# A fused graph and mixture-of-experts layer: routing two places earlier, and the last batch's expert weights fetched only when the expert changes

## The reference

```
xn = layernorm(x)
x  = x + gnn(xn, src, dst, edge_weight) + mix(xn)        # gather by edge, segment sum, linear attention
h  = layernorm(x)
idx = argmax(softmax(h @ gate_w + gate_b))               # one of 8 experts per node
pos = running count of the node within its expert        # kept if pos < C = ceil(1.25 * 12500 / 8)
y   = relu(h @ w1[idx] + b1[idx]) @ w2[idx] + b2[idx]    # 256 -> 1024 -> 256
out = x + where(kept, prob[idx] * y, 0)
```

## Time and profile before

| what | value |
|---|---|
| runs | 2518.9, 2520.43, 2527.71 us |
| median | 2520.43 us |
| the profiled execution | 2522.2 us, of which 2520.3 us lie between its first and last instruction (the span) |
| busy share of the span | PE 82%, DVE 60%, ACT 41%, POOL 72% |
| granted TensorE clock, mean | 0.919 of full speed |
| moved by DMA | 594.32 MB, mean 236 GB/s |
| weight fetches in it | 82 of 1,028 KB and 82 of 1,024 KB |

### The profile page before, as it was taken

One profiled execution on the slowest core, in us unless ns is written; L12 is line 12 of the kernel. 1 busy time (PEld: TensorE's weight loads), 2 busy tenths in 40 slices (PEclk: granted clock), 3 DMA queues, 4 the chain that ended last, 5 costly groups with the idle time before them and its releaser, 6 DMA issues. The chain is left out here.

```text
span 2520.3 us, 42814 instructions
## 1 busy us (share of the span) xinstructions
PE 2056.2 (82%) x12889; PEld 1586.9 (63%) x12889; DVE 1514.9 (60%) x5328; ACT 1036.6 (41%) x2482; POOL 1810.3 (72%) x1888
## 2 busy tenths in 40 slices
PE   0049999994677777899989999998989899796898
PEld 0015656662455556776767777777777777685787
DVE  6676555554457786787646656666556556555233
ACT  4662333331344454553434433443444444342333
POOL 7777777777777777777777777777777777723654
PEclk9968999997788888999989999999999999897999
DMA  9845666664566667777777776777888888775896
GB/s 338 310 142 169 175 173 175 174 174 131 153 197 193 193 198 259 231 240 231 237 229 248 239 229 221 241 236 237 320 280 306 300 316 285 247 260 221 330 349 248
DMA packets 279341, 594.32 MB, mean 236 GB/s; under 512 B 48437, under 2 KB 177214, under 8 KB 256863
## 3 DMA queue, kind: packets, MB, share of 16 engines
q0 software_dynamic: 93168, 256.28, 33.8%
q1 hardware_dynamic: 155553, 284.06, 32.6%
q10 hardware_dynamic: 30390, 51.21, 5.5%
HBM read 506.22 MB, written 87.99 MB: 236 GB/s over the span
## 5 line engine op out<-in xcount | busy, mean ns | idle before, releaser
L931 POOL DMA_INDIRECT rows_sb<-xn_scratch,src_sb x1517 | 1459.0, 962 | 464.2 <-issue 455.8
L1199 PE MATMUL bank<-acc 128*128 128x128 f32 (+1 forms) x2624 | 442.3, 322 | 15.0 <-issue 10.9
L1220 PE MATMUL bank<-acc 128*128 128x256 f32 x1680 | 413.1, 390 | 0.0
L1199 PEld LDWEIGHTS bank<-acc 128*128 128x128 f32 x2624 | 384.9, 204 | 40.8 <-issue 18.6
L1020 PE MATMUL bank<-rows_sb,s_sb 128*24 128x256 f32 x3082 | 225.7, 413 | 202.0 <-DMA rows_sb<-xn_scratch,src_sb 197.4
L1963 ACT ACTIVATE acc<-bank,acc 128x128 f32<-128x128 f32 (+1 forms) x656 | 212.0, 398 | 375.8 <-PE bank L1199 375.7
L1220 PEld LDWEIGHTS bank<-acc 128*128 128x128 f32 x1680 | 313.9, 194 | 49.7 <-issue 0.9
L1484 DVE TENSOR_TENSOR acc<-acc,bank 128x48 f32 x831 | 170.4, 205 | 273.7 <-PE bank L1030 160.4
L1020 PEld LDWEIGHTS bank<-rows_sb,s_sb 128*24 128x24 f32 x3082 | 84.9, 107 | 274.9 <-issue 232.5
L1884 ACT COPY sums<-bank 120x256 f32<-120x256 f32 x208 | 76.5, 368 | 347.2 <-PE bank L1020 347.2
L1915 ACT ACT_TABLE_LOAD x95 | 121.9, 1283 | 194.8 <-PE bank L1109 193.9
(11 more groups left out here) (263 smaller groups left out, 3649.9 us busy)
## 6 DMA issues: line engine op xcount, KB each, us to landing
acc<-ffn_first_in SPq DMA_DIRECT2D x82, 1028.0 KB
acc<-ffn_w_in SPq DMA_DIRECT2D x82, 1024.0 KB
arena<-xn_scratch SPq DMA_DIRECT2D x194, 128.0 KB, 3.2
h_scratch<-arena ACTq DMA_DIRECT2D x97, 256.0 KB
rows_sb<-xn_scratch,src_sb POOLq DMA_INDIRECT x1517
xnt_scratch<-arena SPq DMA_DIRECT2D x97, 128.0 KB, 2.3
arena<-xnt_scratch SPq DMA_DIRECT2D x97, 128.0 KB
arena<-x_in SPq DMA_DIRECT2D x97, 128.0 KB
```

The lines of the kernel that those rows point to most:

```text
L931: pool.indirect_dma_start(out=chunk_row(c), out_offset=None, in_=xn_d, in_offset=bass.IndirectOffsetOnAxis(ap=src_sb[:, c:c + 1], axis=0)) ...
L1199: m = pe.matmul(bank[:, i * tokens:(i + 1) * tokens], w1_sb[k % 2][:, h, f * P:(f + 1) * P], xt[:, k % 2, h, 0:tokens], start=h == 0, stop ...
L1220: m = pe.matmul(bank[:, i * D:(i + 1) * D], hid[:, f, i * P:(i + 1) * P], w2_sb[k % 2][:, f, :], start=False, stop=f == FC - 1 and i == 0)
```

## The change

It has four parts.

1. **Steps.** A tile's steps stand at distances 0, 1, 2, 2, 3, 3, 4, 5 from its entry in place of 0 to 7, and the logits at 6 in place of 8. The row loads on SP move from 2 to 1, the products (step 3) from 3 to 2. On ACT steps 4 and 5 are now in the early part of a place, ahead of the units' relus.
2. **Ticks.** From place 208 on a place takes one tick, except where a batch's sums are made and the place after, which take two; at the sums the first tick stands ahead of them. `last_c` falls from 217 to 215.
3. **Last batch.** Its 18 columns are dealt out in two halves, the first half to the even units and the second to the odd. Units 64 and 65 get their weights from SP as before. For 66 to 81 POOL issues indirect DMAs that read row `expert * 128 + partition`; where the unit two before, which used the same buffer, has the same expert, 1,024 is added to the row, which puts it out of bounds so that nothing is read. DVE works out these rows after `q_ready` and raises `rows_known`.
4. **Kept columns.** Their scatters start at place 209, four a place, and stand ahead of the units' scatters in a place; there are 78 of them.

```
+        STEP_AT = {0: 0, 1: 1, 2: 2, 3: 2, 4: 3, 5: 3, 6: 4, 7: 5}
+        LAP_AT, LOGIT_AT = 3, 6
...
-        chosen_at = [enters[v[-1]] + C_STEPS - 1 for v in routes]
+        chosen_at = [enters[v[-1]] + LOGIT_AT for v in routes]
...
+        def most_ticks(p):
+            return 2 if p < PAIRS or p in sums_at or p - 1 in sums_at else 1
...
-            if ("unit", n - 1) in here or after == len(here):
+            if e_place[n] in sums_at and e_place[n] >= PAIRS and ("unit", n - 1) not in here:
+                here.insert(0, ("unit", n))
+            elif ("unit", n - 1) in here or after == len(here):
...
-        quiet = [p for p in range(PAIRS + 2, last_c + 4) for _ in range(2 + 2 * (p > last_c))]
+        quiet = [p for p in range(PAIRS + 1, last_c + 4) for _ in range(4)]
...
+            def load_new_first(k):
+                col = k - FINAL[0]
+                pool.wait_ge(rows_known, 1)
+                pool.wait_ge(l1_relu, FC * (k - 1))
+                pool.indirect_dma_start(
+                    out=first_sb[k % 2], out_offset=None, in_=ffn_first.rearrange("a p f -> (a p) f"),
+                    in_offset=bass.IndirectOffsetOnAxis(ap=load_row[:, col:col + 1], axis=0),
+                    bounds_check=NE * P - 1, oob_is_err=False).then_inc(new1_ld[k % 2], 16)
...
+                for k in w1_at[p]:
+                    if k in SKIPS:
+                        load_new_first(k)
+                for k in w2_at[p]:
+                    if k in SKIPS:
+                        load_new_second(k)
                 for k in gather_at[p]:
                     gather_unit(k)
...
+                for col in back_at[p]:
+                    scatter_back(col)
                 for k in scatter_at[p]:
                     scatter_unit(k)
-                for col in back_at[p]:
-                    scatter_back(col)
...
+                if b == LAST:
+                    same, row = empty, idf
+                    link(dve.memset(same, 0.0))
+                    link(dve.tensor_scalar(row, expert, float(P), ids[:, 0:1], ALU.mult, ALU.add))
+                    link(dve.tensor_tensor(same[:, 2:n], row[:, 2:n], row[:, 0:n - 2], ALU.is_equal))
+                    link(dve.scalar_tensor_tensor(row, same, float(NE * P), row, ALU.mult, ALU.add))
+                    dve.tensor_single_scalar(load_row[:, 0:n], row, 1.0, ALU.subtract).then_inc(rows_known, 1)
```

More of the change, by code:

```diff
@@ L294, in build @@
         sel = behind(1, 2 * MOST_SLOTS)
+        load_row = behind(1, MOST_SLOTS).bitcast(I32)
         sprb = behind(0, SLOTS)
@@ L509, in queue_value @@
             return sum(i <= b for i in queued)
+        LAST = len(routes) - 1
+        FINAL = [k for k in range(K) if batch_of[k] == LAST]
+        SKIPS = FINAL[2:]
+        assert len(FINAL) % 2 == 0 and LAST in queued
         def small_steps(p, at_end):
@@ L521, in early_steps @@
         def early_steps(p):
-            found = [("logit", t) for t, e in enumerate(enters) if e + 8 == p]
+            found = [("logit", t) for t, e in enumerate(enters) if e + LOGIT_AT == p]
             for b in range(len(routes)):
@@ L546, in build @@
         last_tick = [first_tick[k] + ticks(k) - 1 for k in range(K)]
+        sums_at = [p + 1 for p in chosen_at]
+        def most_ticks(p):
+            return 2 if p < PAIRS or p in sums_at or p - 1 in sums_at else 1
         e_place, time, p = [], 0.0, FIRST_C
-        wanted_at = [slots_at[b] + (4 if slots_at[b] + 4 < PAIRS else 2) for b in batch_of]
+        wanted_at = [min(slots_at[b] + 4, max(slots_at[b] + 2, PAIRS)) for b in batch_of]
         for k, j in e_ticks:
@@ L561, in build @@
                     break
-                if (j > 1 or k == K or p >= wanted) and time >= cost and e_place.count(p) < 2:
+                if (j > 1 or k == K or p >= wanted) and time >= cost and e_place.count(p) < most_ticks(p):
                     time -= cost
@@ L635, in kept_value, with new_value @@
             return 16 * (k // YS + 1)
+        def new_value(k):
+            return 16 * ((k - SKIPS[0]) // 2 + 1)
         def w2_value(k):
@@ L657, in c_steps @@
         def c_steps(p, order):
-            return [(enters.index(p - s), s) for s in order if p - s in enters]
+            return [(enters.index(p - STEP_AT[s]), s) for s in order if p - STEP_AT[s] in enters]
         def first_of(t):
@@ L830, in sync_program @@
                     elif kind == "early":
-                        for t, s in c_steps(k, (2, 0, 3)):
+                        for t, s in c_steps(k, (1, 0)):
                             if s == 0:
                                 load_turned(t)
-                            elif s == 2:
+                            else:
                                 load_rows(t)
-                            elif t + LAP_TILES < T:
-                                load_acc(t + LAP_TILES)
+                        if k - LAP_AT in enters and enters.index(k - LAP_AT) + LAP_TILES < T:
+                            load_acc(enters.index(k - LAP_AT) + LAP_TILES)
                 for k in w1_at[p]:
-                    load_first(k)
+                    if k not in SKIPS:
+                        load_first(k)
                 for k in w2_at[p]:
-                    load_second(k)
+                    if k not in SKIPS:
+                        load_second(k)
                 for k in keep_at[p]:
@@ L975, in scatter_back, with load_new_second @@
                     bounds_check=tokens - 1, oob_is_err=False).then_inc(back_st[s], 16)
+            def load_new_first(k):
[6 more added lines that the diff above has]
+                    bounds_check=NE * P - 1, oob_is_err=False).then_inc(new1_ld[k % 2], 16)
+            def load_new_second(k):
+                col = k - FINAL[0]
+                pool.wait_ge(l2_mm, l1_done(k - 2))
+                pool.indirect_dma_start(
+                    out=flat2(w2_sb[k % 2]), out_offset=None, in_=ffn_w2.rearrange("a p f -> (a p) f"),
+                    in_offset=bass.IndirectOffsetOnAxis(ap=load_row[:, col:col + 1], axis=0),
+                    bounds_check=NE * P - 1, oob_is_err=False).then_inc(new2_ld[k % 2], 16)
             for p in range(PLACES):
@@ L1631, in queue_units @@
                 link(dve.tensor_single_scalar(queue_base, queue_base, float(u1), ALU.max))
-                if u1 > u0:
+                if b == LAST:
+                    half = (u1 - u0) // 2
+                    link(dve.tensor_scalar(sel[:, 0:u1 - u0:2], iota_p[:, u0 + 1:u0 + 1 + half], queue_at, None,
+                                           ALU.is_equal))
+                    dve.tensor_scalar(sel[:, 1:u1 - u0:2], iota_p[:, u0 + 1 + half:u1 + 1], queue_at, None, ALU.is_equal
+                                      ).then_inc(q_selected, 1)
+                elif u1 > u0:
                     dve.tensor_scalar(sel[:, 0:u1 - u0], iota_p[:, u0 + 1:u1 + 1], queue_at, None, ALU.is_equal
@@ L1976, in side_step @@
                 elif kind == "early":
-                    for t, s in c_steps(k, (7,)):
+                    for t, s in c_steps(k, (7, 4, 5)):
                         c_step(t, s)
@@ L1984, in side_step @@
                 elif kind == "late":
-                    for t, s in c_steps(k, (4, 1)):
+                    for t, s in c_steps(k, (1,)):
                         c_step(t, s)
@@ L1990, in scalar_program @@
             for p in range(PLACES):
-                for t, s in c_steps(p, (6, 5)):
+                for t, s in c_steps(p, (6,)):
                     c_step(t, s)
```

30 lines of the change are left out of this document (19 added, 11 removed).

## The result

| | before | after |
|---|---|---|
| median of 20 runs each | 2520.28 us | 2530.35 us (2523.98 to 2536.36) |
| ratio | | 1.0037, 95% interval 1.0028 to 1.0046 |
| the profiled execution, its span | 2522.2, 2520.3 us | 2531.16, 2529.4 us |
| moved by DMA | 594.32 MB | 571.48 MB |

What follows compares the result with a forecast made beforehand. It took POOL as the bound before place 208 and in the last batch. A and B together gain 14.5 us, C costs 7.5, in sum -7: 2513 us, range 2499 to 2531.

Steps and rivals of the forecast that it cites:

- The bound named for the tail: Last batch: POOL binds, at 1.30 us a DMA and seven a unit, 9.1 us against PE's 7.75.
- A: The way to place 208: last pair starts at 2219, last turning at 2231 in place of 2233.55; gain 2.5 us.
- B: The two last routings, up to the last batch's first gather at 2326.1, before 2340.69; gain with A 14.5 us.
- C: The last batch's units, from first gather to end: POOL binds; costs 7.5 us more than before, though 22.6 MB go.
- One sign: Last batch: PE idle 1 to 2 us in every unit, before L1246 or L1270, until unit 78.
- landing takes 2.8: Before place 208: the last row gather, issued at 2216.3, lands in 2.8 us, so the last pair starts at 2219.
- The 17.3 us from sums to table of batch 17: Routing of batch 17: sums to table takes 17.3 us, before 14.3, as DVE has more in between.
- The landing of w1: Last batch, unit 78: 1 MB lands on a nearly empty DMA in 5.5 us, between bounds of 2.8 and 8.8.
- Rival 1: Last batch: POOL doesn't bind and the tail goes at PE's pace, 2502 us; chance 0.22.
- Rival 2: POOL's weight fetches with 8,224-byte row offsets cost 1 us more each, 25 us in all, 2538 us; chance 0.10.
- Rival 3: Squeezed steps stall PE, 2 us a tile over 98 tiles against a slack of 160.7, 2548 us; chance 0.05.
- Rival 4: Out-of-bounds fetches take as long as full ones, so DMA engines bind again beside POOL, about 2522 us; chance 0.08.

Runs made afterwards that it cites:

- few_fetches: The change with POOL issuing only the ten weight fetches that load something, the 22 skipped ones removed; 1.0002 of the kernel before, 2519.5 us.
- rows_first: The change with the last gather of node rows on POOL ahead of the gathers for units 56 and 58; 1.0013 of the kernel before, 2525.8 us.
- dyn_old_steps: The change with last-batch weights loaded by SP behind branches, two read-backs later, last row gather first, steps at old places; 0.9978 of the kernel before, 2518.1 us.
- sp_order_few: The change with only the five needed weight pairs loaded, on SP, and read-backs 6 and 7 two places later; 0.9952 of the kernel before, 2509.6 us.
- undo_steps: The change with the node tiles' steps and logits at their old places, nothing else; 1.0013 of the kernel before, 2524.2 us.
- skip_alone: The kernel before with the third part alone: POOL fetches from unit 66 on, columns in alternating order; 1.0043 of the kernel before, 2530.4 us.

## Why the prediction was wrong

**The bound named for the tail was the right one.** POOL's 1.30 us a DMA and seven a unit over PE's 7.75 are in the rows, the count of 104 DMAs up to w1 of unit 78 came out exactly, and `few_fetches` shows POOL's fetches to be a cause. What failed are terms of the sum: the gather of unit 64 came at 2335.36 and not 2326.1 (A and B, 9.2 us), and from there to the end it took 6.7 us more than forecast (C). One sign failed too: PE was to stand idle 1 to 2 us in every unit until 78, and it stood still at units 70 and 76 only. (Rows 1 also show two slices at 330 to 349 GB/s, not three; nothing rests on it.)

**A, the way to place 208, forecast at a gain of 2.5 us, failed.** The step was "landing takes 2.8, so the last pair starts at 2219". PE started at 2224.07, 5.1 us later: 1.7 because the gather was issued at 2217.97 and not 2216.3, and 3.3 because its rows took 6.1 us. The 2.8 was the median of 48 other gathers, which run between 131 and 191 us, in the start-up. In the change's own trace these have another median,

```profile
acc<-xn_scratch,src_sb POOLq DMA_INDIRECT x48, 5.2
```

and the pair before the last took 6.04 with no unit's gather ahead, so the two transfers of 128 KB, to which I put it in `rows_first`, are not shown to be the reason; what sets this time stays open. From there to the last turning I had 12 us and it was 12.2; it came at 2236.25, not 2231. `rows_first` is worth 6 us for this order. Between executions the stretch before it differs by some us, so I compare means: 2234.6 over the eight kernels with these steps and this order, 2232.4 over the four with the old steps. With a spread of 7 us that shows no gain, and a loss of 2 at most as a hint (one of the four, `dyn_old_steps`, also has the rows first).

**B, routing, forecast with A at 14.5, brought 5.3.** Counted from the last turning it is 8.0 (99.1 us to the gather of unit 64, before 107.1) where I had 12.0. The missing 4 are two terms of 3.9 and 3.6, less 3.6 that the pieces between them took less. From turning to sums of batch 17 I had 19.7 and it was 23.6: ACT's steps stood ahead of the copy of unit 56, 2.52 us of wait, for which I had nothing (before, the wait at this point was 0.56), and a tick at the lower clock. From sums to slots of batch 18 I had 22.4, it was 26.0: DVE took 13.9 us up to the table, not 11.3, and the rest 12.1, not 11.1. The 17.3 us from sums to table of batch 17 came out to the tenth.

**C, 187.3 us from the gather of unit 64, was 194.0.** w1 of unit 78 went 142.5 us behind the gather in place of 138.9: POOL's waits in this stretch, most of them for units 66 and 67, came to 5.0 and not 3.5, and its pace was 1.32 us a DMA and not 1.30, over 104 of them 2.1. From w1 of unit 78 to PE's last matmul it was 39.0, forecast 38.4; that agreement is partly luck, since unit 78 started 6.35 us behind its w1 with no wait for it, and PE's last wait for w1 was at unit 76. From there to the end it was 12.5, forecast 10.0: the last scatter started 4.0 us behind PE's last matmul as before, and the span ended 8.55 behind that start in place of 6.03. The landing of w1, taken as 5.5, was 5.67 from issue to first matmul at unit 70, and the five real fetches of w2 landed after 5.6 to 7.7. DMA: Bandwidth & Descriptors in the Trainium skill, section Anatomy of one DMA, gave 4.4 as an estimate; the trace lies above it, also if the 1.0 us in which POOL makes the DMA is left out (4.7, and 4.6 to 6.7), and the trace decides.

**The rivals.** Rival 1, the tail at PE's pace, did not come: POOL bound it. It also had its size wrong. `few_fetches`, where POOL is no bound, took 2519.5 and not 2502: the waits for units 64 and 65 and the lower clock stay. Removing these two waits in `sp_order_few` was worth 6.3 us, with a new wait of 4.6 in their place. Rival 2 fell: fetches of 8 KB rows take POOL 1.02 and 1.06 us, those that are skipped too.

```profile
L1010 POOL DMA_INDIRECT acc<-ffn_w_in,acc x16 | 16.9, 1055 | 8.1 <-PE bank L1270 4.3 <-issue 3.5 <-ACT acc L2026 0.3
L1002 POOL DMA_INDIRECT acc<-ffn_first_in,acc x16 | 16.2, 1015 | 14.4 <-ACT acc L2026 7.5 <-issue 3.4 <-DVE acc L1799 2.2
```

32 of them are 33 us of POOL's time. The sentence of that page of the Trainium skill (DMA: Bandwidth & Descriptors) that issuing costs a sequencer time that is "usually small relative to the DMA itself" (section Issuing engines are not separate DMA queues) does not hold for them here: taking 22 that move nothing off the queue gave 8.8 us. Rival 3 fell: before 2220 PE's wait for rows and POOL's for PE became

```profile
PE bank L1064 <- DMA rows_sb<-xn_scratch,src_sb: 147.4, 64, 6.8
```
```profile
POOL rows_sb L952 <- PE bank L1064: 2.7, 9, 0.3
```

so PE's slack shrank by 13 us and 147 are left. Rival 4 fell with the DMA share of 0.55.

**What I should have done with the same rows.** I had seen both limits of the tail, SP's read-back ahead of w1 of unit 64 and POOL's seven DMAs. The sum itself holds the kept columns behind the gather, so nothing is counted twice; I did not ask which part of the gain in B pays for them. A gain in time ahead of POOL's full queue is passed on to the end, as `rows_first` shows. The two places that the steps save are another thing: they put nine kept columns behind the gather, 11.8 us, for a chain that is 6.5 us shorter, and `undo_steps` shows that this part of the change loses. The columns need not stand there: POOL stood idle 31.6 us between the first kept column (2255.67) and the gather of unit 64, waiting for DVE, and room for 24 DMAs went unused. That another order would use it was not tried.

## What to carry to other kernels

Before moving work to another queue, count the instructions that the queue then issues per unit against the pace of the engine it feeds; a transfer that is skipped but issued costs the issuing engine all that it ever did. Where a wait on a queue can be late (a read-back that needs other engines' results), put the loads that the critical engine wants ahead of it. And ahead of a saturated queue tell a gain in time from a change of order: rows that came earlier were worth 6 us with the queue full, but steps that moved an item ahead of nine others on it were worth -6 us, and 4 us or more once the queue had room. Last, a landing time belongs to the place in the program where it was measured.

## What the runs showed that I had not expected

- The span ends 5.6 us after the start of the last scatter in the six kernels with squeezed steps and no fetches on POOL, 6.0 in the kernel before, 6.9 in `dyn_old_steps`, 7.1 with ten fetches, and 8.6 to 10.7 with 32 (the change 8.55, `rows_first` 10.1, `skip_alone` 9.9, `undo_steps` 10.7). What keeps it open was not tried.
- The 48 gathers of the start-up landed 2.8 us after issue in the median in the kernel before, 5.2 in the change, and 2.7 to 3.5 in the twelve other kernels; at the last two pairs of the change PE had its rows 6.0 and 6.1 us after the issue.
- A skipped fetch right behind a real one lands with it: w1 of units 71, 73, 77 and 79 landed 4.5 to 6.5 us after their issue, 0.1 to 0.3 behind the w2 ahead of them, where w1 of units 69 and 75 took 2.1.
- A branch, a value load and a counted-up semaphore on SP, twice per unit of 7.75 us, could not be seen in the time: 0.9955 with them, 0.9952 without, each to 0.0015 either way.
